# Row sums of added pairs of exp tiles in a two-batch transformer kernel on one core

## The reference

```python
scores = jnp.einsum('bnqd,bnkd->bnqk', q, k) * scale
scores = jnp.where(causal, -jnp.inf, scores)
attn = jax.nn.softmax(scores, axis=-1)
out = jnp.einsum('bnqk,bnkd->bnqd', attn, v)
...
gated = jax.nn.silu(gate) * up
return jnp.einsum('bsh,dh->bsd', gated, w_down)
```

## Time and profile before

| | us |
|---|---|
| median of 3 runs | 2178.95 |
| lowest, highest | 2174.32, 2179.26 |
| the profiled execution | 2179.44 |
| its span, first to last instruction | 2177.7 |

### The profile page before, as it was taken

How to read it: one execution, slowest core, us unless ns; L and a number is a source line. 1 busy time by engine, 2 the same in 40 slices (tenths; PEclk the granted TensorE clock), 3 DMA queues, 4 the chain that set the end, 5 groups by cost and what they waited for, 6 DMA issues and landing times.

```text
span 2177.7 us, 34223 instructions
## 1 busy us (share of the span) xinstructions
PE 2113.8 (97%) x11056; PEld 1486.4 (68%) x11056; DVE 1253.6 (58%) x2476; ACT 530.9 (24%) x1076; POOL 668.9 (31%) x508
## 2 busy tenths in 40 slices
PE   6999999999999999999989999999999999999998
PEld 5555478888755548888865554888877554588886
DVE  6766564544676647444467665644456767454445
ACT  1344420000144441000014454100011444310001
POOL 3324233332312323323231233333323223233322
PEclk9999999999999999999999999999999999999999
DMA  4333111111323211111242321111113232111113
GB/s 130 94 79 79 31 36 52 49 58 39 79 70 79 70 31 49 50 48 49 68 129 70 79 69 40 39 59 39 49 40 81 68 81 68 40 49 49 59 39 97
DMA packets 59748, 135.15 MB, mean 62 GB/s; under 512 B 10784, under 2 KB 11808, under 8 KB 59552
## 3 DMA queue, kind: packets, MB, share of 16 engines
q1 hardware_dynamic: 59552, 132.71, 21.6%
HBM read 77.62 MB, written 4.19 MB: 38 GB/s over the span
## 4 chain that ended last, share of the span: by engine, by line
PE 88%; issue 5%; DVE 2%; POOL 2%; ACT 1%; DMA 1%; SPq 0%; DVEq 0%; POOLq 0%; ACTq 0%
PE ring L898 13%; PE ring L899 13%; PE ring L900 13%; PE bank L1011 13%; PE ring L965 8%; PE bank L989 7%; PE bank L898 7%; PE bank L900 7%; PE bank L899 7%; PE ring L889 1%; ACT prob L560 1%; DMA area<-nm_lo 1%; POOL area L438 1%; DVE xn L699 1%; POOL prob L463 1%
## 5 line engine op out<-in xcount | busy, mean ns | idle before, releaser
L898 PE MATMUL ring<-xt_hi,area 128*128 128x512 f32 x1248 | 489.8, 392 | 1.1 <-DVE kq_parts L688 1.1
L899 PE MATMUL ring<-xt_lo,area 128*128 128x512 f32 x1248 | 486.4, 390 | 0.0
L900 PE MATMUL ring<-xt_hi,area 128*128 128x512 f32 x1248 | 486.0, 389 | 0.0
L699 DVE CUSTOM_DVE_ANT_0 xn<-ring,mask_row 128x128 bf16<-128x128 f32 (+7 forms) x512 | 374.5, 749 | 99.9 <-PE ring L965 93.9
L560 ACT ACTIVATE prob<-bank 128x512 f32<-128x512 f32 (+3 forms) x768 | 335.0, 489 | 342.4 <-PE bank L989 341.6
L436 POOL TENSOR_SCALAR area<-w_stage 128x1024 fp32r<-128x1024 f32 x131 | 144.4, 1103 | 762.2 <-PE bank L900 404.7
L766 DVE TENSOR_TENSOR prob<-prob,ring 128x512 f32<-128x512 f32 x128 | 87.8, 686 | 456.9 <-ACT prob L578 456.9
L438 POOL TENSOR_TENSOR area<-w_stage,area 128x1024 fp32r<-128x1024 f32 x131 | 322.8, 2464 | 10.9
L578 ACT ACTIVATE prob<-ring 128x512 f32<-128x512 f32 x128 | 76.5, 598 | 970.4 <-PE ring L900 970.4
L898 PEld LDWEIGHTS ring<-xt_hi,area 128*128 128x128 f32 x1248 | 234.3, 188 | 59.1 <-issue 9.8
L900 PEld LDWEIGHTS ring<-xt_hi,area 128*128 128x128 f32 x1248 | 234.3, 188 | 49.1
(11 more groups left out here) (78 smaller groups left out, 2053.4 us busy)
## 6 DMA issues: line engine op xcount, KB each, us to landing
w_stage<-ffn_w SPq DMA_DIRECT2D x96, 512.0 KB, 3.3
area<-kq_parts SPq DMA_DIRECT2D x336, 128.0 KB, 2.4
w_stage<-attn_w SPq DMA_DIRECT2D x35, 512.0 KB, 3.3
x<-x_in SPq DMA_DIRECT2D x24, 256.0 KB, 3.9
area<-attn SPq DMA_DIRECT2D x48, 128.0 KB, 2.3
out<-x SPq DMA_DIRECT2D x16, 256.0 KB, 2.2
bias_rows<-row_bias SPq DMA_DIRECT2D x10, 256.0 KB, 4.2
area<-nm_hi SPq DMA_DIRECT2D x32, 8.0 KB, 1.8
```

The source lines that it names most:

```text
L699: dve.tensor_tensor_reduce(out=sum_out[:, RING[name] % 2, 0:keys], in0=src[:, 0:keys], in1=mask_row[:, TOKENS - keys:], scale=1.0, scalar= ...
L898: pe.matmul(dst, ah, bh, start=first and k == 0, stop=False)
L899: pe.matmul(dst, ah, bl, start=False, stop=False)
L900: ins = pe.matmul(dst, al, bh, start=False, stop=last and k == n - 1)
```

## The change

- The row sums of long units are made of pairs. GpSimd adds exp tile 1 to tile 0, 3 to 2 and 5 to 4 (`add_pair`), each in two halves of two heads, and TensorE makes one group of sums for a pair. Tiles 6 and 7 and all tiles of short units keep a group each. `ADDS_AT` says behind which key tile's mask an addition stands in GpSimd's queue.
- An addition waits for the exps of the second tile, for its mask, and for the weighing of the first tile with the values. The sums of a pair wait for the addition (`pair_added`), and stand two key tiles behind the pair's second.
- `prob` has four buffers. An exp waits for the weighing of the tile four before, and for its addition or sums.
- Scores are issued one head at a time. After head 1 stands the weighing of the tile before, after head 3 the sums that are due, and each of the four places may hold a filling tile.
- The splits of units 5 and 6 go from GpSimd to VectorE, behind their normalisation. The splits of units 0, 1 and 3 stand between the additions and masks of units 5 and 6.
- The copy of one element behind the split of the maximum (L716) goes; the DMAs of `stack_max` wait for the low part itself.
- The filling places of unit 6 go from 0, 2, 4, 6, 10 to 0, 2, 5, 7, 10. The scratch area for software DMAs is smaller, to make room.

```diff
+PROB_BUFS = 4
+PAIRED = (0, 6)
+ADD_PARTS = 2
+ADDS_AT = ({}, {1: (((0, 1), 0), ((0, 1), 1)), 3: (((2, 3), 0),), 4: (((2, 3), 1),), 5: (((4, 5), 0),), 6: (((4, 5), 1),)})
+POOL_SPLITS = UNITS - 3
+SPLIT_ORDER = (0, 1, 2, 4, 3)
...
+            def add_pair(it, u, pair, part):
+                first, second = pair
+                step = J_BASE[u] + second
+                d = second - CT * unit(u)[1]
+                off = max(0, d) * P
+                heads = slice(part * GH // ADD_PARTS, (part + 1) * GH // ADD_PARTS)
+                wait_alone(pool, prob_ready, it * S2_STEPS + GH * (step + 1))
+                if d >= 0:
+                    wait_alone(pool, mask_done, it * UNITS * CT + u * CT + d + 1)
+                wait_alone(pool, pv_done, it * KEY_STEPS + J_BASE[u] + first + 1)
+                dst = prob[:, (step - 1) % PROB_BUFS, heads, off:]
+                pool.tensor_tensor(dst, dst, prob[:, step % PROB_BUFS, heads, off:], ALU.add).then_inc(pair_added, 1)
...
-                    for d in range(CT):
-                        mask_probs(it, u, d)
-                        if u == UNITS - 1 and d == 0:
+                    for w in {6: (2, 4)}.get(u, ()):
+                        split_attn(it, w)
+                    for j in range(key_tiles(u)):
+                        if j >= CT * unit(u)[1]:
+                            mask_probs(it, u, j - CT * unit(u)[1])
+                        for pair, part in ADDS_AT[unit(u)[1]].get(j, ()):
+                            add_pair(it, u, pair, part)
+                        for w in {(5, 1): (0,), (5, 5): (1,), (6, 3): (3,)}.get((u, j), ()):
+                            split_attn(it, w)
+                        if u == UNITS - 1 and j == CT:
                             inverse_deviation(it, 1, 0)
...
-                    if step >= 2:
-                        act.wait_ge(pv_done, it * KEY_STEPS + step - 1)
+                    if step >= PROB_BUFS:
+                        w, i = step_of(step - PROB_BUFS)
+                        group = group_of(w, i)
+                        act.wait_ge(pv_done, it * KEY_STEPS + step - PROB_BUFS + 1)
+                        if i == group[0]:
+                            act.wait_ge(sums_done, summed(it, w, group))
+                        else:
+                            act.wait_ge(pair_added, added(it, w, group))
...
+                                if u - 1 >= POOL_SPLITS:
+                                    split_last(u - 1)
...
+                def sums(u, group):
+                    j = group[0]
+                    step = J_BASE[u] + j
+                    off = max(0, j - CT * unit(u)[1]) * P
+                    if len(group) == 2:
+                        pe.wait_ge(pair_added, added(it, u, group))
+                    for h in range(GH):
+                        rows = slice(h * HEAD, (h + 1) * HEAD)
+                        ins = pe.matmul(den_bank[rows, off:], ones[:, :], prob[:, step % PROB_BUFS, h, off:],
+                                        start=j == 0, stop=group == sum_groups(u)[-1], tile_position=(0, h * HEAD))
+                    ins.then_inc(sums_done, 1)
...
-                        for half, what in enumerate(("values", "sums")):
-                            for own in range(2):
-                                if own == 0:
-                                    scores_t(u, j, 2 * half)
-                                    scores_t(u, j, 2 * half + 1)
-                                else:
-                                    weigh(u, j - 1, what)
+                        for h in range(GH):
+                            scores_t(u, j, h)
+                            if h == WEIGH_AT:
+                                weigh(u, j - 1)
+                            if h == SUMS_AT:
+                                for group in sums_in(u, j):
+                                    sums(u, group)
```

112 lines of the change are left out of this document (62 added, 50 removed).

## The result

The changed kernel took 2203.34 us at the median, the kernel before 2177.73 in the same session: ratio 1.011, 95% interval 1.0092 to 1.0128. Of its four executions one took 11346.64 us and is left out of the ratio; the other three have their median at 2202.78. The forecast was 2163, so its direction was wrong, and the time lies beyond the range. The profiled execution of the changed kernel took 2198.39 us (span 2196.7), 18.95 more than the 2179.44 of before.

A forecast was written before the change was run, and what follows sets the result against it. The prediction took TensorE, busy 97%, as the bound, with VectorE close behind in attention. Terms 20.4 + 5.6 - 3.0 - 3.2 - 3.6 + 1.3 - 1.7 = 15.8 us off 2179.4 gave 2163 us, range 2150 to 2172.

The forecast's parts named there:

- Units 1, 3, 5: Long units 1, 3, 5, twelve in all: fewer row-sum groups gain 1.7 us per unit, 20.4 us together.
- the first part: Key tiles 1 to 3 of units 1, 3, 5: 1.1 us gained per unit, bounds 0 and 2.0.
- the second part: Later key tiles, 4 to 7, of units 1, 3, 5: 0.6 us gained per unit, bounds 0 and 0.78.
- Unit 7: Four in all: 2.5 us gained at key tiles 1 to 4, less 0.2, 0.6 and 0.3: 1.4 each, 5.6 together.
- VectorE's splits: Two attention splits moved to VectorE, units 5 and 6: taken as 0; without cover, 1.1 us four times.
- Unit 5's queue: GpSimd in unit 5: splits among additions make mask 6 and sum (4,5) 0.8 us late, 3.2 us lost together.
- late masks: Tiles 4 and 6 of units 1, 3, 5: TensorE meets masks earlier, 0.25 us lost per unit, 3.0 together.
- Single-head order: Scores issued one by one, each with a filler: 0, give or take a few tenths of a us per unit.
- Clock: Start of unit 7: one more drop of TensorE's clock to half speed, 1.7 us lost.
- rival D: TensorE's clock: thinner streams bring a slow episode into every long unit, 27 us lost, 2190; chance 0.04.
- B: Long units: VectorE takes it all, loads wait for maxima as before; 6.8 us gained, about 6 lost, 2178; chance 0.14.
- C: Long units: GpSimd's queue sets the pace, masks 5, 6, 7 each 1.2 us late, 58 us added, 2193; chance 0.14.

The follow-up runs named there:

- run 5: The kernel before without the row sums of key tiles 1, 3 and 5 in long units, nothing added: 2169.05 us, 0.9953.
- run 15: The changed kernel with old score order, attention splits on GpSimd, units 2 and 4's behind unit 6's first two masks, unit 6's old filling places: 2175.05 us.
- run 16: As run 15, also without pair (4,5), so two pairs in each long unit: 2174.41 us, 0.9978.
- run 13: The base with scores issued head by head, no pairs: 2183.1 us, 1.0022.
- the base: The changed kernel with scores in pairs of heads as before, attention splits where they stood before, and no pairs of tiles: 2178.8 us, 1.0.
- run 14: The base with the attention splits placed as in the change, no pairs: 2201.32 us, 1.0107.

## Why the prediction was wrong, step by step

- **Units 1, 3, 5: 1.7 us gained each.** This term failed: -0.2 to -0.3 came. In the first part I set 9.39 us of TensorE against 9.52 of VectorE and let 0.8 us of idle time stay. But the two don't run side by side: a filling tile waits for a maximum and often a reciprocal in VectorE's queue, and VectorE then waits 0.25 to 1.25 us for the next tile. A key tile went from 3.95 to 3.77, not to about 3.4. The single-head order shares in this: in the old order the same tiles take 3.54 (34.3 for unit 3), as in the run with pairs alone:

```profile
684.76:688.30 3.54, 3.48 (x17) 1.53 (x16) 3.04 (x9) 2.91 (x7) 0.42 (x1) 1.00 0.30 66
688.30:691.84 3.54, 3.48 (x17) 1.53 (x16) 3.42 (x13) 2.18 (x5) 3.54 (x2) 1.00 0.90 207
```

Both take 3.54, with VectorE busy 3.04 in one and 3.42 in the other, so its busy time does not set the step there. Which of the waits does is not shown. In the second part the 0.6 didn't come either: 1.00 us of sums at key tile 7 is paid in full (+0.85) and the 0.78 taken at tile 6 is lost to VectorE (4.30 to 4.36).
- **Unit 7: 1.4 gained.** Measured 1.0 lost. The sums alone give 0.9 there (run 5), the pairs 0.45 to 0.7. Of the 2.5 set for key tiles 1 to 4, 1.4 came, at the first two; step 4 lost its group and kept its 3.44 us. The wait of the sums of pair (2,3) for their addition, 0.5 us, was not in the sum. What turned the sign was the next point.
- **VectorE's splits: 0, "if that cover is gone 1.1 us four times".** This is the step that failed worst. The price was named and the cover believed. The cast and the subtraction took 0.66 + 1.65 us beside GpSimd (0.43 + 0.69 alone, so half of it is the queue and half the port), the negated maximum came that much later, and the ring buffer that it holds stopped the projection: 1.7 us a unit 7 in the changed kernel, 2.0 in the run with splits alone. The row was at hand: a VectorE operation that began beside GpSimd's ended half a microsecond after it. I applied the port to the normalisations (3.6 us) and not to these. The Trainium skill ("SBUF — State Buffer", section "Who interferes with whom") lists `cast` with the operations that can lock the shared ports and calls the blocking complete; the trace agrees: 0.43 us alone against 1.34, and that cast ended 0.29 us after GpSimd's subtraction.
- **Unit 6.** Not in the sum at all. Splits 2 and 4 ahead of the first mask cost 0.5 us in the changed kernel (13.67 to 13.16), 1.2 in the run with the splits alone, and the shifted filling places 0.6 (13.0 to 12.4). I had read the queue of unit 5 alone.
- **Unit 5's queue (3.2) and late masks (3.0).** Small in the changed kernel: unit 5 lost 0.3, and the waits on masks were 19.0 us before and 19.3 after. In the old order unit 5 does vary by 1 us (35.25 to 36.3) with the third pair and not without it. That is neither queue nor mask: from weighing to weighing its steps are the same, and the difference stands ahead of them, where the first score waits for the DMA of the negated maximum. In run 15, in the second and in the fourth iteration:

```profile
729.65 0.72 PE L1057 MATMUL bank<-area 98*128 98x512 f32 x2 [0.34 <-DMA area<-nm_lo]
...
1801.65 0.73 PE L1057 MATMUL bank<-area 98*128 98x512 f32 x2 [1.38 <-DMA area<-nm_lo]
```

The four waits are 1.31, 0.34, 1.00 and 1.38 us with the third pair, and 0.34 or 0.35 with two (run 16). Why that DMA lands later with the third pair is not shown.
- **Single-head order: 0.** It costs 0.1 to 0.2 us in every unit but the last, 4.3 us in all (run 13). Why was not found.
- **Clock: 1.7.** Measured 17 us more at half clock, 8.5 us lost. Of the twelve units 1, 3 and 5 two had a drop, so it was not rival D, which had one in each. Windows about one of the two, at the end of unit 3 of the third iteration (38.1 us instead of 35.0):

```profile
1250.00:1256.00 6.00, 5.31 (x33) 2.85 (x26) 4.55 (x11) 2.19 (x7) 3.65 (x4) 0.99 0.00 1
1256.00:1262.00 6.00, 6.00 (x32) 2.53 (x31) 2.94 (x6) 0.77 (x3) 3.60 (x4) 0.50 0.01 1
```

TensorE is busy 5.31 of 6 us, with loads between that wait up to 0.84 us for maxima, and the grant falls to 0.50 for the next six. The same stretch of the second iteration looks alike and had no drop behind it:

```profile
706.97:712.97 6.00, 5.31 (x33) 2.89 (x26) 4.56 (x11) 2.18 (x6) 3.68 (x4) 1.00 0.00 1
```

The splits bring 20 us of half clock by themselves (23.9 against the base's 3.4), in all their executions: the mean grant is 0.992 to 0.993 with them and 0.997 to 0.999 in the base. The order brings none. Half clock varies between a kernel's executions, and what decides it stays open.
- **Rivals.** B, "VectorE takes it all" (2178), was nearest for the sums in the changed order. C was refuted for units 1, 3 and 5 and cost 0.6 us in unit 7, and D was refuted. None held the mechanism that decided, the moved splits.

The account, by medians: base 2178.8, with the order +4.3, with the splits +22.5, with both 2206.2; the pairs then bring 2.9. The splits' 22.5 are, by the units of run 14, 1.2 us in unit 6 and 2.0 in unit 7 at full clock, 4 x 3.2 = 12.8, and 20.5 us more of half clock, 10.2: 23.0.
